# Four cross-attention blocks in one kernel: the last attention's transposed maxima in a PSUM bank of their own, its maxima ahead of its scores, and a new order of pairs, spreads and output products

## The reference, cut to what matters

```python
# block 0                                    z, u: [B, 128, 256]
q, k, v = split(Wqkv @ z + Winj @ u)         # 16 heads of 64
prob = softmax((q + r_w_bias) . k / 8)       # 256 x 256 per head
x = layernorm_no_affine(Wo @ (prob @ v) + bo + z)
# block 1: 16 heads of 16, 128 latents on 256 keys, then rmsnorm and an MLP (256 -> 1024 -> 256)
# block 2: layer norm, 16 heads of 16, 128 queries on 128 keys, layer norm and an MLP
# block 3                                    16 heads of 8
q, k, v = Wq @ x + bq, Wk @ kv + bk, Wv @ kv + bv
attn = softmax(q . k / sqrt(8))              # 256 x 256 per head
mean, ex2 = attn @ v, attn @ (v * v)
std  = sqrt(relu(ex2 - mean * mean))
out  = (instance_norm(x) * std + mean) * mask
```

## Time and profile before

| | |
|---|---|
| median of 3 runs | 1070.02 us (1069.75 to 1073.35) |
| time of the profiled execution | 1071.41 us |
| its span | 1069.6 us |
| TensorE busy | 928.8 us, 87% of the span |
| VectorE busy | 558.7 us, 52% |
| ScalarE busy | 454.3 us, 42% |
| GpSimd busy | 292.3 us, 27% |
| granted TensorE clock, mean | 0.969 of 2.4 GHz |
| mean DMA rate | 82 GB/s |

### The profile page before, as it was taken

How to read it: one execution, slowest core, us unless ns; L and a number is a source line. 1 busy time by engine, 2 the same in 40 slices (tenths; PEclk the granted TensorE clock), 3 DMA queues, 4 the chain that set the end, 5 groups by cost and what they waited for, 6 DMA issues and landing times.

```text
span 1069.6 us, 20878 instructions
## 1 busy us (share of the span) xinstructions
PE 928.8 (87%) x8304; PEld 592.6 (55%) x8304; DVE 558.7 (52%) x892; ACT 454.3 (42%) x784; POOL 292.3 (27%) x402
## 2 busy tenths in 40 slices
PE   7989988999989988999989998899989999776652
PEld 5566663666546664566636664566646665345421
DVE  3343565445655466445654556555664556553443
ACT  2424443454444544345434545345443554332223
POOL 4230220243201532224202432115212332024101
PEclk9999999999999999999999999999999999997767
DMA  9501313013410324113230234103140123102111
GB/s 369 187 2 40 121 52 128 22 40 143 139 37 9 118 76 138 36 40 132 62 116 19 80 115 137 34 5 126 70 141 29 41 98 112 51 18 78 36 30 40
DMA packets 37447, 87.44 MB, mean 82 GB/s; under 512 B 8552, under 2 KB 26472, under 8 KB 29544
## 3 DMA queue, kind: packets, MB, share of 16 engines
q1 hardware_dynamic: 37352, 86.10, 23.1%
HBM read 77.63 MB, written 8.39 MB: 80 GB/s over the span
## 4 chain that ended last, share of the span: by engine, by line
PE 67%; DVE 16%; issue 7%; ACT 4%; SPq 3%; DMA 2%; POOL 1%; DVEq 0%; ACTq 0%; POOLq 0%
DVE nm L1495 6%; PE GP L1042 6%; PE GP L1053 6%; PE GP L647 5%; PE PV L786 5%; PE GP L649 4%; PE GP L1026 3%; PE SC L769 3%; PE PV L825 3%; PE GP L865 3%; PE PV L973 3%; PE GP L654 2%; PE SC L960 2%; PE MX L702 2%; PE MX L813 2%
## 5 line engine op out<-in xcount | busy, mean ns | idle before, releaser
L1495 DVE TENSOR_REDUCE nm<-MX 128x4 bf16<-128x1024 f32 (+1 forms) x176 | 215.8, 1226 | 145.5 <-PE MX L708 54.5
L1275 ACT ACTIVATE Pr<-SC 128x1024 f32<-128x1024 f32 x128 | 130.8, 1022 | 208.0 <-PE SC L848 128.4
L1841 POOL TENSOR_TENSOR Psum<-Pr 128x512 f32<-128x512 f32 x64 | 83.0, 1298 | 162.8 <-ACT Pr L1275 162.8
L647 PE MATMUL GP<-zP,W 128*128 128x128 f32 x512 | 107.1, 292 | 7.5 <-DMA W<-w 7.5
L649 PE MATMUL GP<-uP,W 128*128 128x128 f32 x512 | 100.5, 279 | 0.0
L647 PEld LDWEIGHTS GP<-zP,W 128*128 128x128 f32 x512 | 79.1, 195 | 28.9 <-issue 27.1
L1304 ACT ACTIVATE Pr<-SC,bcol 128x512 f32<-128x512 f32 x96 | 60.7, 684 | 56.7 <-PE SC L960 56.2
L649 PEld LDWEIGHTS GP<-uP,W 128*128 128x128 f32 x512 | 79.4, 196 | 0.0
L1809 POOL TENSOR_TENSOR stat<-stat,half 128x1 f32<-128x1 f32 x24 | 13.6, 568 | 229.3 <-DVE stat L1683 172.5
L1053 PE MATMUL GP<-WB,work 128*128 128x256 f32 x256 | 62.5, 394 | 10.5 <-DVE work L1625 10.5
L786 PE MATMUL PV<-Pr,V 128*64 128x256 f32 x512 | 69.4, 392 | 0.0
(11 more groups left out here) (205 smaller groups left out, 1671.9 us busy)
## 6 DMA issues: line engine op xcount, KB each, us to landing
W<-w SPq DMA_DIRECT2D x20, 1024.0 KB, 5.1
WA<-w1a SPq DMA_DIRECT2D x8, 1024.0 KB, 7.4
WB<-w1b SPq DMA_DIRECT2D x8, 1024.0 KB, 9.7
WA<-w2a SPq DMA_DIRECT2D x8, 1024.0 KB, 4.8
WB<-w2b SPq DMA_DIRECT2D x8, 1024.0 KB, 6.9
Kx<-k_parts SPq DMA_DIRECT2D x24, 192.0 KB
...
```

Source lines behind the costliest of these rows:

```text
L647: pe.matmul(dst, W0[:, piece, 2 * s, at:at + P], zP[:, s * P:s * P + P], start=True, stop=False)
L1275: act.activation(Pr[:, n % 4:n % 4 + 2, :], SCP[:], ACT.Exp, scale=8.0 ** -0.5 if L else 0.125)\
L1495: dve.tensor_reduce(dst, MXP[:].rearrange("p i (a k) -> p i a k", a=a), AX_X, ALU.max, negate=True)\
L1841: pool.tensor_tensor(Psum[:, c % 4, :].rearrange("p (a l) -> p a l", l=D), two[:, :, 0:D], two[:, :, D:2 * D], ALU.add)\
```

## The change

The transposed maxima of the last attention leave `MX`. T3(g) goes into the `GP` bank of "u1" (`shift_rows3`, `turned3`), group g at its own quarter of the bank. It signals `t3_full`, and the copy to `Qx` signals `s_T3`. T3(0) waits until that bank is free (`s_Q3`), each later T3 for the copy of the one before, S3 for the copy of its group, and P3(4), the first product into "u1", for all four copies.

The table `BOTH` is new. The M3 pairs stand one to three steps earlier. B(1) stands two steps later and B(2) one, and O(1) to O(5) one to three steps later, so that O(5) to O(7) end the stage together. `rest` is issued by VectorE after the reduce of M0(3,2), and the middle and the low term ("terms") after the reduce of M3(0,0), where all three stood ahead of both. ScalarE issues `queries3` one step earlier. For b = 7 (`ENTRY`) the order of the units is as before, and only the bank of T3 is different. No instruction is added or removed on TensorE, ScalarE, VectorE or the DMA queues. The number of matmuls, copies and bytes stays.

```diff
@@ -65,18 +65,17 @@
...
-ENTRY = [(3, 0, 0), (3, 0, 2), (3, 0, "T")]
+ENTRY = [("rest", 0), ("terms", 0), (3, 0, 0), (3, 0, 2), (3, 0, "T")]
...
 BOTH = [(0, 0, [], []), (0, 1, [], []), (0, 2, [], []), (0, 3, [], []),
-        (0, 4, [(0, 3, 2)], [("den", 1), (0, 3, "T"), ("recip", 0, 0), ("recip", 0, 1)]),
-        (0, 5, [(3, 0, 0)], []), (0, 6, [(3, 0, 2)], []), (0, 7, [("den", 2), (3, 0, "T")], [(3, 1, 0)]),
-        (3, 0, [], [(3, 1, 2)]),
-        (3, 1, [("den", 3), (3, 1, "T"), ("recip", 1, 0)], [(0, 0, "B")]),
-        (3, 2, [(0, 1, "B"), ("recip", 1, 1)], [("out", 0), (3, 2, 0)]),
-        (3, 3, [("out", 1), (3, 2, 2)], [("out", 2), ("out", 3), (3, 2, "T")]),
-        (3, 4, [(0, 2, "B")], [(3, 3, 0)]),
-        (3, 5, [(3, 3, 2), ("out", 4)], [("out", 5), (3, 3, "T")]),
-        (3, 6, [(0, 3, "B")], []), (3, 7, [("out", 6), ("out", 7)], [])]
+        (0, 4, [(0, 3, 2), ("rest", 0)], [(3, 0, 0)]),
+        (0, 5, [("den", 1), ("terms", 0), (0, 3, "T"), ("recip", 0, 0)], [(3, 0, 2)]),
+        (0, 6, [], [("recip", 0, 1), (3, 1, 0)]), (0, 7, [(3, 0, "T"), (3, 1, 2)], [("den", 2), (3, 2, 0)]),
+        (3, 0, [], [(3, 2, 2), ("den", 3), (3, 1, "T")]), (3, 1, [(0, 0, "B")], [(3, 2, "T")]),
+        (3, 2, [(3, 3, 0), ("out", 0)], [("recip", 1, 0)]), (3, 3, [(3, 3, 2)], []),
+        (3, 4, [("recip", 1, 1)], [(0, 1, "B"), (3, 3, "T"), ("out", 1)]),
+        (3, 5, [("out", 2), (0, 2, "B")], []), (3, 6, [("out", 3)], [(0, 3, "B"), ("out", 4)]),
+        (3, 7, [("out", 5), ("out", 6), ("out", 7)], [])]
@@ -97,7 +96,7 @@
...
-        for L, g, u in (name for name in names if name[0] in range(4)):
+        for L, g, u in (name for name in names if name[0] in range(4) and (name[0], name[2]) != (3, "T")):
@@ -499,7 +499,11 @@
             ending.end()
 
         def shifts(b, L, g):
-            return nmT_ready, SHIFTS.index((b, L, g)) + 1
+            return (s_T3, 4 * b + g + 1) if L == 3 else (nmT_ready, SHIFTS.index((b, L, g)) + 1)
+
+        def turned3(b, g):
+
+            return GP[order_of(b).at("u1")[0]][:].bitcast(BF16)[:, g * D:g * D + D]
 
@@ -731,22 +735,31 @@
                             if j == per - 1:
                                 mm.then_inc(mx_full[i], 1)
 
+                def shift_rows3(g):
+                    pe.wait_ge(mx_done, reduced(MX_AT[b, 3, g, 3]))
+                    if g == 0:
+                        pe.wait_ge(*order_of(b).bank_taken("u1"))
+                    else:
+                        pe.wait_ge(s_T3, 4 * b + g)
+                    for s in range(2):
+                        mm = pe.transpose(turned3(b, g)[:, s * P:s * P + P], nm3[:, g % 2, s, :], identb[:])
+                    mm.then_inc(t3_full, 1)
+
...
                     wait(pe, *mx_bank_taken(n))
                     pe.wait_ge(mx_done, reduced(MX_AT[b, L, g, steps - 1]))
-                    if L in (0, 3):
+                    if L == 0:
                         for s in range(2):
-                            mm = pe.transpose(rows_out[:, s * P:s * P + P], (nm3 if L else nm0)[:, g % 2, s, :],
-                                              identb[:])
+                            mm = pe.transpose(rows_out[:, s * P:s * P + P], nm0[:, g % 2, s, :], identb[:])
                     else:
@@ -859,7 +872,7 @@
                 if k == 0:
                     pe.wait_ge(s_V3, b + 1)
                 if g % 2 == 0 and kc == 0:
-                    pe.wait_ge(*o.bank_taken(name))
+                    pe.wait_ge(*(o.bank_taken(name) if k == 0 else (s_T3, 4 * b + NG)))
                 for s in range(HG):
                     j, e = divmod(s, 2)
@@ -1274,10 +1287,10 @@
                     pr_taken(act, n + 1, 1)
                     act.activation(Pr[:, n % 4:n % 4 + 2, :], SCP[:], ACT.Exp, scale=8.0 ** -0.5 if L else 0.125)\
                         .then_inc(p_ready, 2)
-                    if b >= 0 and L == 0 and k == 5:
-                        queries3(b)
                     if L == 0 and (k in (4, 6) or k == 2 and b < 0):
                         evacuate(b + 1, k // 2 - 1)
+                    if b >= 0 and L == 0 and k == 4:
+                        queries3(b)
@@ -1468,18 +1481,16 @@
 
             def maxima(b, L, g, u):
 
+                if (L, u) == (3, "T"):
+                    dve.wait_ge(t3_full, 4 * b + g + 1)
+                    src = turned3(b, g)[96:100].unsqueeze(1).unsqueeze(1).to_broadcast([HG, 2, 2, D])
+                    dve.tensor_copy(group(Qx[96:100], g), src).then_inc(s_T3, 1)
+                    return
...
-                    turned = MX[n % 2][:].bitcast(BF16)
-                    if L == 0:
-                        dst, src = nmT0[:, g % 2, :], turned[:, 0:D]
-                    elif L == 3:
-                        dst = group(Qx[96:100], g)
-                        src = turned[96:100, 0:D].unsqueeze(1).unsqueeze(1).to_broadcast([HG, 2, 2, D])
-                    else:
-                        dst, src = nmT[:, g, :], turned[:, 0:P]
-                    dve.tensor_copy(dst, src).then_inc(nmT_ready, 1)
+                    dst, w = (nmT[:, g, :], P) if L else (nmT0[:, g % 2, :], D)
+                    dve.tensor_copy(dst, MX[n % 2][:].bitcast(BF16)[:, 0:w]).then_inc(nmT_ready, 1)
                     return
@@ -1501,6 +1512,13 @@
                 def unit(L, g, u=None):
                     if L == "recip":
                         reciprocals0(b + 1, g, u)
+                    elif L == "rest":
+                        rest(take(order_of(b), "q3"), "bq", rest_q, (s_Q3h, b + 1)).then_inc(s_Q3r, 1)
+                    elif L == "terms":
+                        dve.wait_ge(s_Q3r, b + 1)
+                        dve.tensor_copy(parts[:, 1, :], rest_q).then_inc(s_Q3m, 1)
+                        dve.wait_ge(s_Q3m, b + 1)
+                        dve.tensor_tensor(parts[:, 2, :], rest_q, parts[:, 1, :], ALU.subtract).then_inc(s_Q3l, 1)
@@ -1735,12 +1753,6 @@
                     ins = dve.tensor_scalar(Q3b[:, t, :], g[:, 0:D], col("bq"), hmask[:, 4 + t:5 + t],
                                             ALU.add, ALU.mult)
                 ins.then_inc(s_Q3b, 1)
-                rest(g, "bq", rest_q, (s_Q3h, b + 1)).then_inc(s_Q3r, 1)
-                dve.wait_ge(s_Q3r, b + 1)
-                dve.tensor_copy(parts[:, 1, :], rest_q).then_inc(s_Q3m, 1)
-                dve.wait_ge(s_Q3m, b + 1)
-                dve.tensor_tensor(parts[:, 2, :], rest_q, parts[:, 1, :], ALU.subtract).then_inc(s_Q3l, 1)
-
                 mixed(b, range(4, 16) if more else range(8))
```

5 lines of the change are left out of this document (3 added, 2 removed).

## The result

The changed kernel takes 1037.38 us (median of 4 runs, 1034.84 to 1038.79), against 1071.68 us for the kernel before, run beside it on the same chip (4 runs, 1069.75 to 1074.32). The ratio is 0.9676, with a 95% interval of 0.9642 to 0.9709. A second measurement of the same pair gave 1038.17 us (1036.73 to 1042.31) and 0.970 (0.9677 to 0.9723). The forecast was 1039, in a range of 1032 to 1053.

A forecast was written before the change was run, and what follows sets the result against it. TensorE's work plus its waits, mostly for the MX banks, bound the merged stages. Seven stages at 4.7 us plus 0.3 for b = 7 gave 33.2, less 2 for Qx, 31.2 us: 1039 us, range 1032 to 1053.

The forecast's parts named there:

- the stage's gain: Merged stages: TensorE's waits shrink while its work stays the same, 4.7 us less per stage, 32.9 us in seven.
- The term for `Qx`: S3(0) in merged stages: terms end 2.87 us later, so it waits for Qx, 0.3 us per stage, 2 us in all.
- MX is the bottleneck, and T3 leaves it: Merged stage: MX uses fill 30.3 of some 34 us; moving the four T3 out takes away 4.4 us.
- the table of starts: One merged stage worked item by item from M0(3,2) to P3(6): four waits left, stage 4.8 us shorter.
- M3(0,0) gains by the terms' move: Start of merged stage: the reduce of M0(3,2) goes ahead of the terms, leaving M3(0,0) a wait of 0.61 us.
- What was costed at nothing: Loads behind Qx have some 20 us to spare; copies, reciprocals and queries3 fit in time: no cost.
- b = 7, 0.3 us: Last attention alone: order kept, only a pair that waited for a copy gains, 0.31 us.
- The two rivals with weight: Qx lands late, waiting 2.2 us in each stage, 1052 us (10 in 100); the waits move, 1053 us (5 in 100).
- The rival on the slower side: S3(0) waits for Qx more than the stage gains, landing over 12.9 us after the last term; 2 in 100.

The follow-up runs named there:

- run with other neighbours: Changed kernel with T3(1) ahead of D(3) and T3(2) ahead of P3(0): 1040.95 us, ratio 0.971.
- run with the hold: Changed kernel where SyncE issues the loads behind those of Qx only once Qx has landed: 1036.57 us, ratio 0.9676.
- run with the bank alone: Kernel before, in its old order, with T3(0) to T3(2) in the step's own bank and T3(3) left in MX: 1070.37 us, ratio 0.9991.

## Why the prediction was right

The mechanism is shown step by step. One term of the sum was clearly mis-sized, the stage's gain, since one step of its working, "the work of TensorE stays the same", is false. The term for `Qx` was right within the spread of executions.

- **MX is the bottleneck, and T3 leaves it.** Right. The waits of a stage fell from 5.6 to 1.26 us, and three of those left stand at the places and have the sizes that the table of starts gave. It was right for a reason that the prediction stated only in part. It priced T3's bank and the new order in one sum, and the runs show that most of the gain belongs to neither alone: 0.1 and 1.5 us of 5.4.
- **The stage's gain, 4.7 us.** Mis-sized. It measured 5.4 without S3(0)'s wait, outside its own 4.2 to 5.2. The waits gave 4.3, and 4.7, as forecast, when each is counted with the 0.07 us of overlap that it costs, as the prediction counts from start to start. These lost overlaps stand in the trace as work, and are some 0.35 of the 1.06 us by which the work fell: the run with T3 left in MX has the same order and five more waits, and 37.04 us of work instead of 36.75. The other 0.7 us are the order, and here "the work of TensorE stays the same" is false: the table took one start-to-start time for each kind of item, and it is one for each pair of neighbours. From M3 to S0 it was 0.43 us where the table had 0.54, and from T3 to S3 0.12 where it had 0.20. The run with other neighbours moved two of these pairs and got back some 0.2 us of work.
- **Qx comes late, 2 us in all.** The right mechanism, and near in size: waits of 3.2 us in one profile and 2.3 in the other, at S3(0), put to the DMA. But they are no chance spread over seven stages of 0.3 us. The stores are 1.3 us late in three elements, where a code load meets them. The loads have a spread of their own. By the completions in the trace of the kernel before, `Qx` landed 7.4 to 9.3 us after the last term in its seven merged stages, with every store on time. The prediction had the one record in which a matmul waited (landed after 7.7 us, S3(0) at 7.95), and a spread of 1.8 us is more than its margin of 0.14. The Trainium skill, DMA: Bandwidth & Descriptors, section "Latency and other measured facts", allows each access to memory to grow from 0.2 to 2 us at high load. The growth here came in b = 2 at a mean of 41 GB/s, and in b = 3 there was none at 73, so the load that the trace measures is not what made these stores late.
- **M3(0,0) gains by the terms' move.** Right: 0.61 us as worked out, and 1.77 with the terms in their old place.
- **What was costed at nothing.** The loads behind `Qx` on SyncE's queue: right, even held back by another 4.4 us they are on nobody's path (no change in the run with the hold). The copies, reciprocals and `queries3`: no wait is put to them.
- **b = 7, 0.3 us.** Not seen: 34.35 us before, 34.47 after. A term this small is beyond what two executions show.
- **b = 0.** Its stage was 1.95 us longer than its neighbours before, at a clock of 0.50 for some 3 us of it, and took 38.13 us at full clock after. The prediction's 7 x 4.7 counted it as one of seven. Since the run with the bank alone has a stage of 43.74 us there at full clock, the old order does not force the drop, and about 2 us of the 36.6 may be of that one execution alone. How often others have it stays open.

The net result, 36.6 us of span against a sum of 31.2, is made up of 7 x 0.67 = 4.7 us more from the stages and 2 us more from b = 0's clock, 0.4 less from b = 7, 1.2 less from `Qx`, and 0.4 outside the stages. By the medians the gain is 34.3 us, 3.1 more than the sum. That the forecast of 1039 missed 1037.38 by only 1.6 is in part luck: it started from the median of three runs of the kernel before, 1070.02, where four have 1071.68.

The two rivals with weight fell by their own marks. `Qx` was late in three stages by 0.7 to 1.4 us, not by 2.2 in each. The waits did not move but went. The rival on the slower side needed a landing 12.9 us behind the last term. The longest in the changed kernel was 9.5, and 10.3 in the new order with T3 in MX. Yet its mechanism is real, and nearer than I had it: 3.4 us of delay in the terms took 32 us of span back, of which 19 are more waits of S3(0) and 10 what its seven stages lost through the clock.
